# Self-attention scores of the second batch from stacked high and low parts (48 rows a head), one decoder layer on one core

## The chip, the cores and the metric

The kernel runs on one NeuronCore of a Trainium2 chip. The metric is the device time of one execution in microseconds (us), as a median of several runs. The engines are named PE (TensorE, matrix products), DVE (VectorE), ACT (ScalarE), POOL (GpSimd) and SP (SyncE, which here only issues DMAs). They run their own instruction streams in order and wait for each other through semaphores.

## The reference

One pre-norm decoder layer in float32, for x of shape (2, 256, 256): causal self-attention with 16 heads of 16, an attention over a context of 512 tokens, and a mixture of 16 experts of which 4 count for each token.

```python
def _L0_attn_ref(X, Wq, bq, Wk, bk, Wv, bv, Wo, bo):
    scale = 1.0 / np.sqrt(np.sqrt(16))
    Q = (X @ Wq.T + bq).reshape(B, S, 16, 16) * scale
    K = (X @ Wk.T + bk).reshape(B, S, 16, 16) * scale
    V = (X @ Wv.T + bv).reshape(B, S, 16, 16)
    scores = jnp.einsum('bqhd,bkhd->bhqk', Q, K)
    scores = jnp.where(causal, scores, -jnp.inf)
    attn = jax.nn.softmax(scores, axis=-1)
    return jnp.einsum('bhqk,bkhd->bqhd', attn, V).reshape(B, S, 256) @ Wo.T + bo

x = x + attn(layernorm(x))
x = x + context_attention(layernorm(x), ctx_2048, mask)
x = x + experts(layernorm(x))
```

## The kernel before

Everything stays in SBUF; DMAs bring inputs and expert weights. The core does the projections, then self-attention in 16 steps, then context attention, then 16 experts.

**High and low parts.** Most products are not taken in float32. Each operand is split into a high part (rounded to float32r, the format of the names kh, qh, XH, WHg) and a low part (the rest, kl, ql, XL, WLg), and a product is the sum of three: high by high, low by high, high by low. The keys' high parts are written by ACT (L419), their low parts by POOL (`low_keys`, L321); the queries' high parts by ACT (L424), their low parts by DVE (L623).

**The 16 steps.** A step v takes two heads j = 0, 1 of one batch: steps 0 to 7 are the first batch, 8 to 15 the second. Two steps make a group of four heads. Heads are 16 wide and lie two by two in strips of 32 partitions. The queries are stored twice, each copy with zeros over one head of every strip (`parity`), so a product over the 32 rows of a strip gives one head's scores. PE, ACT and DVE each have a loop over v:

- PE: `scores(v)`, then `turn(v-1)` (transposes of the exponentials), and in odd steps `values` (the product with V). Scores are for the 256 queries of a batch in two blocks of 128: the first block sees 128 keys and is one float32 product (L970), the second sees 256 keys and is the three part products (L974). The two heads lie in different strips of the array and their products run side by side.
- DVE: mask and row maximum (L718, two instructions and two read-outs per head), then the copy of one head's turned exponentials out of PSUM (L743), besides other work that is placed at fixed steps.
- ACT: the exponentials (L438, four per step), the copy of the other head (L486), in odd steps the copy of a group's output (L493).

Scores of step v go to one of three pairs of PSUM banks, and the turned exponentials of step v take the same banks, so `scores(v)` waits for the copies of step v-3 (`pt_done`). `turn(v-1)` waits for the exponentials of step v-1 (`exp_done`).

From step 10 on the first batch's output is also finished inside these steps: `turn_back` (L1008), `outputs` (L649, L650), the transposes of att (L904), `project` (L1017), `residual` (L656), `centre` (L664 to L668). After step 15 follow the context scores (L1029) with their row maximum (L681).

**Order by hand.** There is no scheduler: each engine's order is the code's. POOL does constants, the sum xb (L301), the keys' low parts, then the splits of the first two experts' weights (L356, L308, L360, L315), of the router (L340, L342) and of the context (L350, L352), the mask (L331, L334) and from then on the reciprocal deviations (`rstds`, L296). SP issues all input DMAs but three, the last being dbias (L247), and then waits in a loop for buffers of expert weights (L253, L255).

Of the kernel before, what the change touches and what calls it, by code (L numbers as in the profile page):

```python
# [36 lines left out]
DW = D * KD  # L37

# [4 lines left out]
def decoder_layer(nc, x_d, ctx_d, ctxT_d, wqkv_d, wo_d, params_d, rows_d, mask_d, dbias_d, we_d, out_d):  # L43
    ctx = ExitStack()
    with ctx:
# [7 lines left out]


# [98 lines left out]
        qh, ql = ([X[1][:, m, :].rearrange("p (r b q) -> p r b q", r=2, b=B) for m in range(KD)] for X in (HH, HL))  # L153
        q2 = [qpar[:, m, :, :].rearrange("p r (b c q) -> p r b c q", b=B, c=QC)[:, :, :, QC - 1, :] for m in range(KD)]
# [45 lines left out]
        out_done = sem("out_done")  # L200

# [32 lines left out]
        def _(sp):  # L234
# [12 lines left out]
            sp.dma_start(dbias[:, :], dbias_d).then_inc(dbias_in, 16)  # L247
            with sp.Fori(1, E // 2) as pair:
# [13 lines left out]
        def _(pool):  # L262
# [27 lines left out]
            g.memset(vp[:, :, :, DH:HP], 1.0)  # L290

# [69 lines left out]

            low_keys(0)
# [26 lines left out]
        def _(act):  # L389
# [75 lines left out]
            for v in range(NV + 2):  # L465
# [6 lines left out]
                if v == NV - 2:  # L472
# [5 lines left out]
                    a.activation(pt[:, w // 2 % 2, 2 * (w % 2), :, :].rearrange("p c q -> p (c q)"),  # L478
                                 PS[:, 2 * (w % 3), 0:BLK * P], ACT.Copy).then_inc(pt_done[0], 1)
                if 1 <= v <= NV:  # L480
# [5 lines left out]
                    a.activation(pt[:, w // 2 % 2, 2 * (w % 2) + 1, :, :].rearrange("p c q -> p (c q)"),  # L486
# [80 lines left out]
        def _(dve):  # L567
# [141 lines left out]
            for v in range(NV + 2):  # L709
# [27 lines left out]
                if 1 <= v <= NV and v != NV - 2:  # L737
# [5 lines left out]
                    v_.tensor_copy(pt[:, w // 2 % 2, 2 * (w % 2), :, :].rearrange("p c q -> p (c q)"),  # L743
# [152 lines left out]
        def _(pe):  # L896
# [56 lines left out]
            def scores(v):  # L953
# [4 lines left out]
                if v in (0, 4):  # L958

                    pe.wait_ge(kl_done, g + 1)  # L960
                    pe.wait_ge(ql_done, g + 1)
                if v == 2:
                    pe.wait_ge(k_done, KD)
                if v >= 3:
# [3 lines left out]
                tiles = [slice(HP * (2 * pair + j), HP * (2 * pair + j + 1)) for j in range(2)]  # L968
# [280 lines left out]
```

## Time and profile before

| what | value |
|---|---|
| median of 3 runs | 222.13 us (221.68 to 222.31) |
| the profiled execution, its own time | 221.69 us |
| its span | 219.6 us |
| PE busy | 212.3 us (97%) |
| DVE busy | 159.5 us (73%) |
| ACT busy | 129.7 us (59%) |
| POOL busy | 84.2 us (38%) |
| DMA | 17.41 MB, mean 79 GB/s |

The span is the stretch between the first and the last instruction that the profiler saw; the execution's own time is 2.1 us longer. PE's busy time is modelled, and matmuls overlap, so 97% does not mean that PE has no room. The granted clock was full speed (2.4 GHz) in all 40 slices of the page.

### The profile page before, as it was taken

The numbers are of one execution on the slowest core, as the hardware profiler recorded it, in microseconds if no ns is written. First come the engines' busy times: TensorE is split into PE (matmuls) and PEld (weight loads), VectorE is DVE, ScalarE is ACT, GpSimd is POOL, SyncE is SP. The second block draws the span as 40 slices with busy tenths as digits, with TensorE's granted clock in tenths as the row PEclk, the third lists the DMA queues.
The fourth block names the chain that finished last, engine by engine and source line by source line (L and its number), as shares of the span: only waits on it lengthen the run. The fifth ranks groups of instructions, "written<-read, shape, count | busy, mean of one in ns | idle before, by whom it ended". The sixth has DMA issues, their size and how long they took to land.

```text
span 219.6 us, 4392 instructions
## 1 busy us (share of the span) xinstructions
PE 212.3 (97%) x1394; PEld 176.9 (81%) x1394; DVE 159.5 (73%) x438; ACT 129.7 (59%) x248; POOL 84.2 (38%) x70
## 2 busy tenths in 40 slices
PE   7999999998999999999999999999999999999995
PEld 2688766776776789788898898898898898898893
DVE  3579897879468558898895785785786786786754
ACT  2238789859632714656765665675676666666340
POOL 6259989201002010246535615615516516416000
PEclk9999999999999999999999999999999999999999
DMA  6994420000000000031442142142241241310002
GB/s 181 328 383 152 145 100 0 0 4 0 3 0 0 3 0 1 0 87 61 145 143 87 60 143 72 72 143 54 89 143 40 103 143 28 115 48 0 0 0 96
DMA packets 7997, 17.41 MB, mean 79 GB/s; under 512 B 928, under 2 KB 3120, under 8 KB 7856
## 3 DMA queue, kind: packets, MB, share of 16 engines
q1 hardware_dynamic: 7552, 16.94, 23.7%
q10 hardware_dynamic: 432, 0.31, 0.5%
q8 instruction: 7, 0.11, 0.2%
q14 instruction: 6, 0.05, 0.1%
HBM read 16.72 MB, written 0.52 MB: 79 GB/s over the span
## 4 chain that ended last, share of the span: by engine, by line
PE 88%; DVE 5%; ACT 3%; issue 3%; POOL 1%; DVEq 0%; ACTq 0%; POOLq 0%
PE PS L1160 37%; PE PS L1176 20%; PE PS L932 3%; PE PS L1044 3%; PE PS L1029 3%; PE PS L984 3%; PE PS L920 2%; PE PS L1127 2%; ACT pr L438 2%; PE PS L1017 2%; PE PS L946 2%; PE PS L970 2%; PE PS L1205 2%; PE PS L997 2%; PE PS L974 1%
## 5 line engine op out<-in xcount | busy, mean ns | idle before, releaser
L308 POOL TENSOR_TENSOR WLg<-raw_g,WHg 128x1024 fp32r<-128x1024 f32 x16 | 38.3, 2396 | 70.8 <-ACT WHg L408 70.6
L1160 PE MATMUL PS<-XH,WHg 128*128 128x512 f32 x120 | 47.0, 391 | 0.0
L1160 PE MATMUL PS<-XL,WHg 128*128 128x512 f32 x120 | 46.9, 391 | 0.0
L1160 PE MATMUL PS<-XH,WLg 128*128 128x512 f32 x120 | 46.7, 389 | 0.0
L840 DVE TENSOR_SCALAR pt<-pt 128x512 f32<-128x512 f32 x30 | 25.0, 833 | 22.4 <-ACT pt L532 22.4
L1176 PE MATMUL PS<-WHd,HH 128*128 128x256 f32 x120 | 34.0, 283 | 0.0
L1176 PE MATMUL PS<-WLd,HH 128*128 128x256 f32 x120 | 34.0, 283 | 0.0
L1176 PE MATMUL PS<-WHd,HL 128*128 128x256 f32 x120 | 34.0, 283 | 0.0
L532 ACT ACTIVATE pt<-PS,bup 128x512 f32<-128x512 f32 x30 | 20.7, 688 | 15.2 <-PE PS L1160 15.2
L538 ACT ACTIVATE HH<-pt 128x512 fp32r<-128x512 f32 x30 | 18.9, 629 | 16.1 <-DVE pt L844 15.7
L438 ACT ACTIVATE pr<-masked,nmax 128x128 f32<-128x128 f32 x64 | 23.7, 444 | 5.9 <-DVE nmax L718 5.9
L529 ACT ACTIVATE pt<-PS,params 128x512 f32<-128x512 f32 x30 | 20.6, 688 | 10.8 <-PE PS L1160 10.8
L1160 PEld LDWEIGHTS PS<-XH,WLg 128*128 128x128 f32 x120 | 22.5, 188 | 4.8
L1160 PEld LDWEIGHTS PS<-XH,WHg 128*128 128x128 f32 x120 | 22.6, 188 | 4.2
L1160 PEld LDWEIGHTS PS<-XL,WHg 128*128 128x128 f32 x120 | 22.6, 188 | 4.1
L844 DVE SCALAR_TENSOR_TENSOR pt<-pt 128x512 f32<-128x512 f32 x30 | 22.4, 746 | 4.2 <-ACT pt L529 2.0
L833 DVE SCALAR_TENSOR_TENSOR x<-PS,score,x 128x256 f32<-128x256 f32 x60 | 24.8, 476 | 0.0
L1176 PEld LDWEIGHTS PS<-WHd,HH 128*128 128x128 f32 x120 | 23.0, 191 | 0.9 <-issue 0.3
L1176 PEld LDWEIGHTS PS<-WHd,HL 128*128 128x128 f32 x120 | 23.0, 191 | 0.5
L1176 PEld LDWEIGHTS PS<-WLd,HH 128*128 128x128 f32 x120 | 23.0, 191 | 0.0
L718 DVE CUSTOM_DVE_ANT_0 masked<-PS,causal 128x128 f32<-128x128 f32 x64 | 18.9, 353 | 4.2 <-PE PS L974 4.2
L849 DVE TENSOR_TENSOR HL<-pt,HH 128x512 fp32r<-128x512 f32 x30 | 20.6, 688 | 1.4
(162 smaller groups left out, 355.8 us busy)
## 6 DMA issues: line engine op xcount, KB each, us to landing
raw_g<-we_d SPq DMA_DIRECT2D x16, 512.0 KB, 4.0
raw_w<-we_d SPq DMA_DIRECT2D x16, 256.0 KB, 2.7
ctxT<-ctxT_d SPq DMA_DIRECT2D x1, 1024.0 KB, 10.4
ctx_sb<-ctx_d SPq DMA_DIRECT2D x1, 1024.0 KB, 12.5
wqkv<-wqkv_d SPq DMA_DIRECT2D x3, 256.0 KB, 4.9
out_d<-x SPq DMA_DIRECT2D x4, 128.0 KB, 1.8
rows<-rows_d SPq DMA_DIRECT2D x1, 264.0 KB, 6.3
x<-x_d ACTq DMA_DIRECT2D x2, 128.0 KB, 3.0
```

The lines of the kernel that those rows point to most:

```text
L308: g.tensor_tensor(WLg[slot][:, :, :, :].rearrange("p k g f -> p (k g f)"), raw_g[slot][:, :], WHg[slot][:, :, :, :].rearrange("p k g f -> ...
L438: i = a.activation(pr[:, v % 2, j, cols], masked[:, v % 2, j, cols], ACT.Exp, bias=nmax[:, v % 2, j, qc:qc + 1], scale=-1.0)
L529: a.activation(glu[:, m, :], PS[:, 2 * m, :], ACT.Gelu_apprx_sigmoid, bias=gub[:, bass.ds(e, 1), 0, m]).then_inc(glu_done, 1)
L532: a.activation(upc[:, m, :], PS[:, 2 * m + 1, :], ACT.Identity, bias=bup1[:, bass.ds(e, 1), m]).then_inc(up_done, 1)
L538: a.activation(HH[slot][:, m, :], hid[:, m, :], ACT.Copy).then_inc(hh_done, 1)
L718: i = v_.tensor_tensor_reduce(out=masked[:, v % 2, j, cols], in0=PS[:, 2 * (v % 3) + j, cols], in1=causal[:, cols], scale=1.0, scalar=HUGE ...
L833: v_.scalar_tensor_tensor(out=acc[:, c, :], in0=PS[:, 4 + 2 * slot + c // 2, (c % 2) * D:(c % 2 + 1) * D], scalar=score[:, c, bass.ds(e, 1 ...
L840: v_.tensor_scalar(upc[:, m, :], upc[:, m, :], 1.0 - LIMIT, 1.0 + LIMIT, ALU.max, ALU.min).then_inc(upc_done, 1)
L844: v_.scalar_tensor_tensor(out=hid[:, m, :], in0=glu[:, m, :], scalar=GLU_MAX, in1=upc[:, m, :], op0=ALU.min, op1=ALU.mult).then_inc(hid_do ...
L849: v_.tensor_tensor(HL[slot][:, m, :], hid[:, m, :], HH[slot][:, m, :].bitcast(F32), ALU.subtract).then_inc(hl_done, 1)
L1160: i = t.matmul(PS[:, 2 * m + part, :], w[slot][:, k, part, m * P:(m + 1) * P], xx[:, k, :], start=(n == 0), stop=(n == 3 * KD - 1))
L1176: i = t.matmul(PS[:, 4 + 2 * slot + c // 2, (c % 2) * D:(c % 2 + 1) * D], hh[slot][:, k, c * P:(c + 1) * P], w[slot][:, k, :], start=(n == ...
```

## The change

Only the second batch's scores (steps 8 to 15) are computed in another way. For each of its heads the 16 rows of the three operand parts are stacked in 48 partitions: keys as low, high, high, and queries as high, high, low. One product over 48 rows is then the sum of the three. Heads 0 to 3 of a group of eight stand in partitions 0 to 47, heads 4 to 7 in 64 to 111, in the free dimension one after another. The first block of 128 queries is taken from the same stacks and is no longer a float32 product. The stacks are built by way of DRAM, by SP: six DMAs write the parts of 8 heads, and after all six have landed four DMAs read them back into `raw_ks` and `raw_qs`; this is done for each half m of the heads. POOL then rounds the stacks into `ks` and `qs` (the same memory) with two casts for each half, and PE waits for them in steps 8 and 12. POOL also clears `raw_ks` and `raw_qs` at the start. Queries of the second batch are no longer stored twice; their high and low parts get instructions of their own. In the first batch the two heads of a step come from strips 0 and 2 or 1 and 3, and no longer from 0 and 1 or 2 and 3.

```diff
+            sp.wait_ge(parts_zero, 2)
+            for m in range(KD):
+                sp.wait_ge(kl_done, m + 1)
+                for a, part in enumerate((kl[m], kh[m], kh[m])):
+                    sp.dma_start(k_parts[m, :, a], part[:, S:T].bitcast(F32)).then_inc(parts_out, 16)
+                sp.wait_ge(ql_done, 2 * m + 2)
+                for a, part in enumerate((qh1[m], qh1[m], ql1[m])):
+                    sp.dma_start(q_parts[m, :, a], part.bitcast(F32)).then_inc(parts_out, 16)
+                sp.wait_ge(parts_out, (m + 1) * 2 * PARTS3 * 16)
+                for rows_of, parts in ((raw_ks, k_parts), (raw_qs, q_parts)):
+                    for j in range(2):
+                        sp.dma_start(rows_of[64 * j:64 * j + PARTS3 * DH, m * NG:(m + 1) * NG, :],
+                                     parts[m, j * NG:(j + 1) * NG].rearrange("t a d n -> (a d) t n")).then_inc(parts_in[m], 16)
...
+            g.memset(raw_ks[:, :, :], 0.0).then_inc(parts_zero, 1)
+            g.memset(raw_qs[:, :, :], 0.0).then_inc(parts_zero, 1)
...
+            def take_parts(m):
+                pool.wait_ge(parts_in[m], 4 * 16)
+                for whole, raw in ((ks, raw_ks), (qs, raw_qs)):
+                    g.tensor_copy(whole[:, m * NG:(m + 1) * NG, :], raw[:, m * NG:(m + 1) * NG, :]).then_inc(parts_done, 1)
...
             low_down(0, 0)
+            take_parts(0)
             high_gate_up(1)
             low_gate_up(1, 1)
+            take_parts(1)
             split_router()
...
             def high_queries(m):
-                act.wait_ge(q_done, m + 1)
-                for r in range(2):
-                    i = a.activation(qh[m][:, r], q2[m][:, r], ACT.Copy)
-                i.then_inc(qh_done, 1)
+                act.wait_ge(q_done, 2 * m + 1)
+                a.activation(qh[m], q2[m], ACT.Copy).then_inc(qh_done, 1)
+                act.wait_ge(q_done, 2 * m + 2)
+                a.activation(qh1[m], q1[m], ACT.Copy).then_inc(qh_done, 1)
...
                 for r in range(2):
-                    i = v_.tensor_scalar(qpar[:, m, r, :], PS[:, Q_BANK[m], :], bq[:, m:m + 1], parity[:, r:r + 1], ALU.add, ALU.mult)
+                    i = v_.tensor_scalar(qpar[:, m, r, 0:S], PS[:, Q_BANK[m], 0:S], bq[:, m:m + 1], parity[:, r:r + 1], ALU.add, ALU.mult)
                 i.then_inc(q_done, 1)
+                v_.tensor_scalar(q1[m], PS[:, Q_BANK[m], S:T], bq[:, m:m + 1], -DH ** -0.25, ALU.add, ALU.mult).then_inc(q_done, 1)
 
             def low_queries(m):
-                dve.wait_ge(qh_done, m + 1)
-                v_.tensor_tensor(ql[m], q2[m], qh[m].bitcast(F32), ALU.subtract).then_inc(ql_done, 1)
+                for n, (low, q, high) in enumerate(((ql[m], q2[m], qh[m]), (ql1[m], q1[m], qh1[m]))):
+                    dve.wait_ge(qh_done, 2 * m + n + 1)
+                    v_.tensor_tensor(low, q, high.bitcast(F32), ALU.subtract).then_inc(ql_done, 1)
...
+                if v in (2 * NG, 3 * NG):
+                    pe.wait_ge(parts_done, 2 * g + 2)
...
+                if b == 1:
+                    whole = [slice(64 * j, 64 * j + PARTS3 * DH) for j in range(2)]
+                    t4 = g * NG + pair * 2 + r
+                    for out, tile in zip(outs, whole):
+                        t.matmul(out[:, P:BLK * P], qs[tile, t4, P:S], ks[tile, t4, :], start=True, stop=True)
+                    for out, tile in zip(outs, whole):
+                        t.matmul(out[:, 0:P], qs[tile, t4, 0:P], ks[tile, t4, 0:P], start=True, stop=True).then_inc(sc_done, 1)
+                    return
```

On PE, step 8 (the first of the second batch) and the turn of step 7 before the change; each row is an instruction with its destination, sources and size:

```order
L970 MATMUL PS<-kT,qpar 128x128 [waits pt_done1,pt_done0]
L970 MATMUL PS<-kT,qpar 128x128
L974 MATMUL PS<-HH 128x256 x2
L974 MATMUL PS<-HH,HL 128x256 x2
L974 MATMUL PS<-HL,HH 128x256 x2
L984 MATMUL PS<-ident,pr 128x128 [waits exp_done]
```

The same place on PE after the change:

```order
L1012 MATMUL PS<-ks,qs 128x256 [waits pt_done1,pt_done0,parts_done]
L1012 MATMUL PS<-ks,qs 128x256
L1014 MATMUL PS<-ks,qs 128x128 x2
L1031 MATMUL PS<-ident,pr 128x128 [waits exp_done]
```

Eight products became four, and the first of them waits for POOL's casts as well.

On POOL, the place behind the low part of the first expert's down weights, after the change (before it, the casts into ks and qs are not there, and the rest follows in the same order):

```order
L343 TENSOR_TENSOR WLd<-raw_w,WHd 128x512 [waits whd_done]
L394 CAST ks<-raw_ks 128x1024 [waits parts_in0]
L394 CAST qs<-raw_qs 128x1024
L384 CAST WHg<-raw_g 128x1024 [waits raw_g_in1]
L336 TENSOR_TENSOR WLg<-raw_g,WHg 128x1024 [waits whg_done]
L394 CAST ks<-raw_ks 128x1024 [waits parts_in1]
L394 CAST qs<-raw_qs 128x1024
L368 CAST router_parts<-params 128x2x16 [waits param_in]
```

Four casts entered POOL's order, two of them in front of the second expert's weights, and the splits of router, context and mask moved behind all four.

## Rows read from the trace of the kernel before

**Rows 1.** The page: busy us, share of the span and instructions of each engine.
```profile
PE 212.3 (97%) x1394; PEld 176.9 (81%) x1394; DVE 159.5 (73%) x438; ACT 129.7 (59%) x248; POOL 84.2 (38%) x70
```

**Rows 2.** Timeline of PE: start us, length us, engine, line, operation, count.
```profile
33.27 0.49 PE L970 MATMUL PS<-kT,qpar 32*128 32x128 f32 x4
33.52 0.37 PE L974 MATMUL PS<-HH 32*128 32x256 f32 x2
33.72 0.29 PE L974 MATMUL PS<-HH,HL 32*128 32x256 f32 x2
33.84 0.29 PE L974 MATMUL PS<-HL,HH 32*128 32x256 f32 x2
34.05 0.88 PE L984 MATMUL PS<-ident,pr 128*128 128x128 f32 x6
...
37.64 0.49 PE L970 MATMUL PS<-kT,qpar 32*128 32x128 f32 x4
```

**Rows 3.** Timeline of ACT, steps 8 to 10 (in brackets: idle time before, its releaser).
```profile
34.83 1.49 ACT L438 ACTIVATE pr<-masked,nmax 128x128 f32<-128x128 f32 x4
...
36.59 1.48 ACT L438 ACTIVATE pr<-masked,nmax 128x128 f32<-128x128 f32 x4
...
38.35 0.36 ACT L493 ACTIVATE osum<-PS 128x256 f32<-128x256 f32 x1
39.20 1.49 ACT L438 ACTIVATE pr<-masked,nmax 128x128 f32<-128x128 f32 x4 [0.48 <-DVE nmax L718]
```

**Rows 4.** Timeline of DVE, step 10, and the context's first row maximum.
```profile
38.52 0.29 DVE L718 CUSTOM_DVE_ANT_0 masked<-PS,causal 128x128 f32<-128x128 f32 x1 [1.12 <-PE PS L974]
...
56.31 0.69 DVE L681 CUSTOM_DVE_ANT_0 qpar<-PS,pen 128x512 f32<-128x512 f32 x1 [1.38 <-PE PS L1029]
```

**Rows 5.** The chain that ended last, in order of time, steps 10 to 16.
```profile
38.13 0.40 PE PS L974 x5
...
40.38 0.43 DVE att L650
...
43.55 0.42 PE PS L970 x4
...
54.45 1.69 PE PS L1029 x6
```

**Rows 6.** Timelines of PE and of DVE up to the first step's maximum.
```profile
15.70 0.29 PE L974 MATMUL PS<-HL,HH 32*128 32x256 f32 x2
...
16.13 0.29 DVE L718 CUSTOM_DVE_ANT_0 masked<-PS,causal 128x128 f32<-128x128 f32 x1
```

**Rows 7.** Timeline of POOL.
```profile
3.66 0.95 POOL L290 MEMSET vp<- 128x1024 f32 x1
9.54 2.81 POOL L301 TENSOR_TENSOR xb<-x,rows 128x256 f32<-128x256 f32 x4 [4.93 <-DMA rows<-rows_d]
...
23.14 1.03 POOL L356 CAST WHg<-raw_g 128x1024 fp32r<-128x1024 f32 x1
...
26.56 0.21 POOL L340 CAST router_parts<-params 128x32 fp32r<-128x32 f32 x1
...
37.52 2.37 POOL L352 TENSOR_TENSOR keys_low<-ctxT,keys_high 128x1024 fp32r<-128x1024 f32 x1
```

**Rows 8.** Stretches: us and length, busy of each engine, granted clock, DMA share, GB/s.
```profile
0.00:5.00 5.00, 3.62 (x9) 1.35 (x10) 1.42 (x4) 1.28 (x1) 3.48 (x17) 1.00 0.59 168
18.00:20.00 2.00, 2.00 (x21) 1.57 (x20) 2.00 (x7) 2.00 (x7) 1.92 (x2) 1.00 0.41 143
```

**Rows 9.** The page: packets, MB, share of 16 engines; KB and us to landing.
```profile
q1 hardware_dynamic: 7552, 16.94, 23.7%
...
out_d<-x SPq DMA_DIRECT2D x4, 128.0 KB, 1.8
```

**Rows 10.** Timeline of SP: start and length of issues.
```profile
5.50 0.55 SPq L242 DMA_DIRECT2D raw_w<-we_d  x1
8.51 3.62 SPq L247 DMA_DIRECT2D dbias<-dbias_d  x1
```

More of the change, by code:

```diff
@@ L37 @@
 DW = D * KD
+STEPS = 2 * NG
+PARTS3 = 3
 def decoder_layer(nc, x_d, ctx_d, ctxT_d, wqkv_d, wo_d, params_d, rows_d, mask_d, dbias_d, we_d, out_d):
@@ L52, in decoder_layer @@
         PS = ctx.enter_context(nc.psum_tensor("PS", [P, 8, 512], F32))
+        raw_parts = ExitStack()
+        raw_ks, raw_qs = (raw_parts.enter_context(nc.sbuf_tensor(n, [P, STEPS, S], F32)) for n in ("raw_ks", "raw_qs"))
+        raw_parts.close()
+        ks, qs = (sb(n, [P, STEPS, S], F32R) for n in ("ks", "qs"))
+        k_parts, q_parts = (nc.dram_tensor(n, (KD, G8, PARTS3, DH, S), F32, kind="Internal").ap() for n in ("k_parts", "q_parts"))
         first_use = ExitStack()
@@ L152, in decoder_layer @@
         kh, kl = ([X[0][:, m, :] for m in range(KD)] for X in (HH, HL))
-        qh, ql = ([X[1][:, m, :].rearrange("p (r b q) -> p r b q", r=2, b=B) for m in range(KD)] for X in (HH, HL))
-        q2 = [qpar[:, m, :, :].rearrange("p r (b c q) -> p r b c q", b=B, c=QC)[:, :, :, QC - 1, :] for m in range(KD)]
+        qh, ql = ([X[1][:, m, 0:2 * P].rearrange("p (r q) -> p r q", r=2) for m in range(KD)] for X in (HH, HL))
+        qh1, ql1 = ([X[1][:, m, S:T] for m in range(KD)] for X in (HH, HL))
+        q2 = [qpar[:, m, :, S - P:S] for m in range(KD)]
+        q1 = [qpar[:, m, 0, S:T] for m in range(KD)]
         keys_flat = qpar[:, :, :, :].rearrange("p k r t -> p (k r t)")
@@ L200, in decoder_layer @@
         out_done = sem("out_done")
+        parts_zero, parts_out, parts_done = sem("parts_zero"), sem("parts_out"), sem("parts_done")
+        parts_in = [sem(f"parts_in{m}") for m in range(KD)]
         XS_BANK, XT_BANK, XV_BANK = (7, 2, 4, 5), (3, 4, 6, 3), (1, 2, 4, 5)
@@ L477, in _ @@
                     act.wait_ge(pt_done[0], w)
[L478 removed]
+                    a.activation(pt[:, w // 2 % 2, w % 2, :, :].rearrange("p c q -> p (c q)"),
                                  PS[:, 2 * (w % 3), 0:BLK * P], ACT.Copy).then_inc(pt_done[0], 1)
@@ L967, in scores @@
                 outs = [PS[:, 2 * (v % 3) + j, :] for j in range(2)]
-                tiles = [slice(HP * (2 * pair + j), HP * (2 * pair + j + 1)) for j in range(2)]
+                if b == 1:
[6 more added lines that the diff above has]
+                    return
+                tiles = [slice(HP * (pair + 2 * j), HP * (pair + 2 * j + 1)) for j in range(2)]
                 for out, tile in zip(outs, tiles):
-                    t.matmul(out[:, 0:P], qpar[tile, g, r, b * S:b * S + P], kT[tile, g, b * S:b * S + P],
-                             start=True, stop=True)
+                    t.matmul(out[:, 0:P], qpar[tile, g, r, 0:P], kT[tile, g, 0:P], start=True, stop=True)
                 for n, (q, k) in enumerate(((qh, kh), (ql, kh), (qh, kl))):
                     for out, tile in zip(outs, tiles):
-                        i = t.matmul(out[:, P:BLK * P], q[g][tile, r, b, :], k[g][tile, b * S:(b + 1) * S],
+                        i = t.matmul(out[:, P:BLK * P], q[g][tile, r, :], k[g][tile, 0:S],
                                      start=(n == 0), stop=(n == 2))
@@ L1067, in _ @@
                 if v == 3:
-                    pe.wait_ge(q_done, KD)
+                    pe.wait_ge(q_done, 2 * KD)
                     project_values(1)
```

6 lines of the change are left out of this document (3 added, 3 removed).

## Prediction

> **What bounds the kernel now.** I read the page first: PE is marked busy for 97% of the span [rows 1], which looks as if every product removed were time gained. Its busy time is modelled, though, so the second view is the timelines of PE, ACT and DVE side by side over steps 8 to 10, and the question at each gap is who waits for whom. A step's scores hold PE from 33.27 to 34.05, 0.78 us [rows 2]. DVE starts on them 0.88 after they began (37.64 to 38.52 in step 10) [rows 2, 4], ACT's exponentials start 0.68 after that (39.20) [rows 3]. ACT itself has no idle time in steps 8 and 9: exponentials at 34.83 and 36.59, the output copy until 38.71; only before 39.20 does it wait, 0.48 us for DVE [rows 3]. So the steps run as a ring (scores, maximum, exponentials, turn, scores), in which ACT is nearly the bound. The chain of waits in order of time is the third view: from step 10 to the context scores at 54.45 it goes through PE and through DVE (att at 40.38) by turns [rows 5]. After 54.45 nothing is changed, and what is gained there should be carried to the end.
>
> **The change, part by part.**
>
> *Scores of steps 8 to 15.* Eight products become four. Before, the part products of 256 columns for two heads follow each other at 0.20 and 0.12 us (33.52, 33.72, 33.84), and the last pair takes 0.29 from its start [rows 2]. After, a pair of 256 columns comes first and the pair of 128 starts 0.12 to 0.20 behind it and ends 0.28 later; DVE picks up 0.03 after that. So DVE starts 0.43 to 0.52 after PE, where it was 0.88; I take 0.48, a gain of 0.40 per step on the path from PE to DVE. On PE itself some 0.4 of 0.78 go. No row shows a product over 48 rows nor one of 128 columns in float32r; bounds are 0 (if such pairs ran one after the other and at a slower rate, they would last as long as what they replace) and 0.53 (below). Added over eight steps this would be 3.2 us, and nearly all of it is hidden:
>
> - Steps 8 and 9: DVE's maximum would be earlier, but the exponentials cannot be, as ACT has work without a gap until 38.71. Gain 0. The turns and the values product wait for those exponentials, so step 10's scores start at 37.64 as before.
> - Step 10: DVE starts at 37.64 + 0.48 = 38.12 instead of 38.52, and ACT at 38.80 instead of 39.20; ACT is free at 38.71. Gain 0.40.
> - Steps 11 to 15: now DVE's order binds. Its maximum of step 11 stands behind the finished outputs of the first batch (att at 40.38 in the chain [rows 5]), which themselves moved by the same 0.40; later it stands behind the residual rows, then behind the centring. PE waits in between for ACT's copy of the turned att. Each of these instructions is unchanged, so the shift of 0.40 is handed on and not added to: scores that come earlier wait for a busy DVE. Even with the shortest products the shift can't pass some 0.53, since PE's turn of step 9 waits for exponentials that end at 38.07 (36.59 + 1.48) [rows 3], and the first batch's turning back stands behind it.
>
> *Prologue.* DVE writes the queries in three instructions of 256 columns instead of two of 512, and the low parts in two instead of one. The first step's products end at 15.70 + 0.29 = 15.99, DVE takes them at 16.13 without idle time [rows 6]: DVE was late by 0.1 at most. Gain 0 to 0.1; I take 0.05.
>
> *Clearing the stacks.* Two memsets of 2048 columns, twice 0.95 each: 3.8 us, in POOL's idle 4.93 us before xb [rows 7]. Cost 0; were the cover gone, the excess would delay the keys' low parts and so step 0.
>
> *DMAs.* SP's new DMAs stand behind dbias, whose issue took 3.62 us, so the queue is full there, and before the loads of experts 2 and on, whose buffers are wanted only in the expert stage. The write of one part is 128 runs of 1 KB. In the first 5 us, where such runs are loaded, 0.59 of 16 engines moved 168 GB/s [rows 8]: 17.8 GB/s each, 0.057 us for 1 KB. Call that p. The mean packet of the queue took 0.237 x 16 x 219.6 / 7552 = 0.110 us for 2.2 KB [rows 9], so p lies between 0.05 and 0.11; I take 0.057, as the row with the same size. What a write needs besides is 1.8 - 8 x 0.057 = 1.3 us from the row of out_d [rows 9]. The engines are full of loads until about 18.2 (share 0.41 in 18 to 20) [rows 8]. The writes' DRAM side has 8 as its outermost size; whether 8 or 16 engines carry one no row shows, and I reckon with 8, the slower.
> First half: 768 packets over 8 engines 96p = 5.5, landed at 18.2 + 5.5 + 1.3 = 25.0. Four reads: issues of 0.55 each [rows 10] make 2.2, the last one's data 12p = 0.7, and 1.3: 29.2. POOL, at its place since 23.14, waits 6 us, then two casts of 1.03 [rows 7]: 31.3. PE needs them at 33.27: 2.0 to spare.
> Second half: SP is free at 27.2; 0.55 + 5.5 + 1.3 + 4.2 bring it to 38.8; casts to 40.9. Needed in step 12, at 43.55 - 0.4 = 43.1 [rows 5]: 2.2 to spare.
> *POOL behind them.* Router, context and mask splits took from 26.56 to 39.89, 13.3 us: they end at 54.2. The first batch's context keys are needed at 54.0 and are among the first of these; the reciprocal deviation behind all of them is needed by DVE before its maximum at 56.31 - 0.4 [rows 4, 7]. 1.7 remain for one small instruction. Cost 0.
>
> **Sum.** 0.40 + 0.05 = 0.45 off the profiled execution's 221.69 gives 221.24. That execution lies 0.44 under the median of the runs, and a comparison is made with medians: 222.13 - 0.45 = 221.7.
>
> **The rivals.**
>
> *The stacks come late (slower).* With p free, the first half is ready at 25.1 + 108p and the second at 29.2 + 204p. The second is late from p = 0.068, the first from 0.076; at p = 0.080 step 12 starts 2.4 late, everything after it as well: 222.13 - 0.45 + 2.4 = 224.1. At the queue's mean of 0.110 it would be 8.5 late. For it: the two round trips are in series, and the margin is 2 us of some 20. Against: the rows of 1 KB runs. It rests on the 8 engines: with 16 the second half is ready at 29.2 + 108p, in time even at 0.110.
> The Trainium skill, page "DMA: Bandwidth & Descriptors", section "Why a DMA increments its semaphore by 16 and not by 1", says that a DMA goes over the largest number of engines up to 16 that divides the outermost size of both sides. By that rule the writes go over 8 engines and the reads over 16; no row here shows it.
>
> *Nothing gained.* Pairs over 48 rows don't run side by side, or 128 columns of float32r are as slow as float32's, which took 0.25 for the pair (33.27 to 33.52) [rows 2]. Then DVE starts 0.6 to 0.9 after PE, and the time is 222.1. For it: no row has this form. Against: pairs over 32 rows do run side by side, 512 columns in 0.12 us.
> The Trainium skill, page "TensorEngine Tiling (Array Packing)", section "Tiling Modes", has two independent tiles of 64 rows; by it the pairs run side by side and this rival falls.
>
> *PE counts after all (faster).* In the chain PE's scores stand again in step 12 (43.55) [rows 5], and the ring's even steps (10, 12, 14, and 16's context scores) could each give 0.4: 222.13 - 4 x 0.4 = 220.5. For it: PE's share of the span. Against: the walk above, where DVE is busy when those scores come.
>
> **How the numbers follow.** A measurement of this kernel tells 0.3% (0.67 us) from no change: faster is below 221.5, slower above 222.8. My forecast of 221.7: 0.32. Nothing gained, 222.1: 0.15. PE counts after all, 220.5: 0.28. Stacks late, 224.1: 0.20, with 0.05 more for a POOL that ends later than reckoned. So faster 0.29 (with 0.01 from the edge of the forecast), same 0.46, slower 0.25. The forecast's own range is 221.5 to 222.1; the range for 8 in 10 runs from 220.5 to 223.6, which leaves out most of the late stacks.
>
> **What the profile after would show.** Right: DVE's first maximum of step 10 starts near 0.48 after its scores; ACT still without a gap in steps 8 and 9; DVE without idle time before its maxima of steps 11 to 15; context scores at 54.0; POOL's first cast into ks at about 29, the third at about 39; no wait of PE for POOL in steps 8 and 12. Wrong: PE idle in step 8 or 12 with a cast as releaser (late stacks); DVE starting 0.6 or more after the new products (nothing gained); DVE idle before its later maxima and context scores before 53.4 (PE counts).

## The result, and the profile after

| what | before | after |
|---|---|---|
| median of 6 runs each, same chip | 222.01 us (221.60 to 222.31) | 226.78 us (224.34 to 227.45) |
| ratio, with its 95% interval | | 1.0195 [1.0154, 1.0235] |
| the profiled execution, its own time | 221.69 us | 224.34 us |
| its span | 219.6 us | 222.6 us |
| granted clock over the span | 1.00 (profiled execution) | 0.992 in two runs (224.34, 224.51), 0.983 to 0.985 in four (226.63 to 227.45) |

The change makes the kernel slower by 4.8 us. The prediction said 221.7, within 220.5 to 223.6; even the fastest run lies outside. The profiled execution is one of the two short ones, so it shows a loss of 2.65 us only. No run near the median was profiled, and the experiments had to stand in for it.

The page after, first the head and the busy times [rows 1], then the granted clock in the 40 slices:

```profile
span 222.6 us, 4327 instructions
PE 210.9 (95%) x1346; PEld 175.3 (79%) x1346; DVE 162.4 (73%) x442; ACT 129.9 (58%) x248; POOL 91.3 (41%) x76
PEclk9799999999999999999999999999999999999999
```

PE has less work (48 records and 1.4 us less; a float32 product leaves two records) and the execution is longer. The digit to stop at is the 7 in the granted clock's second slice; before, all 40 were 9.

**The prologue.** DVE's timeline after, from the layer norm to its first copy (start us, length us, engine, line, operation, count; in brackets idle time before and its releaser):

```profile
3.57 1.52 DVE L614 BATCH_NORM_STATS2 stats<-x 128x6 f32<-128x256 f32 x4 [3.57 <-DMA x<-x_d]
5.13 0.38 DVE L637 BATCH_NORM_AGGREGATE mv<-stats 128x2 f32<-128x6 f32 x4
6.17 3.03 DVE L629 TENSOR_SCALAR xn<-x,mv,rstd 128x256 f32<-128x256 f32 x4 [0.67 <-ACT rstd L436]
```

POOL's timeline after, the same stretch:

```profile
3.65 0.95 POOL L316 MEMSET vp<- 128x1024 f32 x1
4.55 1.80 POOL L317 MEMSET raw_ks<- 128x2048 f32 x1
6.29 1.80 POOL L318 MEMSET raw_qs<- 128x2048 f32 x1
```

Four instructions into xn take 3.03 us, where they took 1.38 before (the row `6.06 1.38 DVE L593` of that trace). DVE is shown as busy, not as idle, so no view of waits names the cause. Taken one by one, one of the four lasts 2.07 us and the others some 0.40; it is the first, since 8.24 to 9.20 is just the time of the other three. It was held from 6.17 to the end of POOL's second memset at 8.09, past the change of memsets at 6.3. PE pays for it, as its timeline after shows:

```profile
8.39 1.90 PE L942 MATMUL PS<-ident,xn 128*128 128x128 f32 x8 [2.03 <-DVE xn L629]
10.21 2.13 PE L970 MATMUL PS<-xT,wqkv 128*128 128x256 f32 x5
...
18.10 0.60 PE L1018 MATMUL PS<-kT,qpar 32*128 32x128 f32 x6
```

and the stretches of that time (us and length, busy of PE, weight load, DVE, ACT and POOL with counts, granted clock, DMA share, GB/s):

```profile
9.00:10.00 1.00, 1.00 (x7) 0.89 (x5) 0.21 (x1) 0.53 (x1) 0.46 (x1) 0.50 1.06 410
10.00:11.00 1.00, 1.00 (x4) 0.73 (x3) 0.68 (x2) 0.07 (x1) 1.00 (x3) 0.50 1.03 412
```

The transposes start at 8.39 instead of 6.62, 1.77 late. After the 2.03 us in which PE stood still the granted clock is 0.50 (1.2 GHz) from 9 to 11 us and 0.57 from 11 to 12, and the lateness grows to 2.96: step 0's scores start at 18.10, not 15.14. The clock's share of this is 1.19 us, since in a_again (below), the same program, the transposes also start at 8.39, the clock stays at 1.00 and step 0 starts at 16.91.

**The changed stage.** PE's timeline after, the scores of step 8 and of step 10 [rows 2]:

```profile
36.26 0.38 PE L1012 MATMUL PS<-ks,qs 48*128 48x256 f32 x2
36.48 0.22 PE L1014 MATMUL PS<-ks,qs 48*128 48x128 f32 x2
...
40.45 0.39 PE L1012 MATMUL PS<-ks,qs 48*128 48x256 f32 x2
40.67 0.22 PE L1014 MATMUL PS<-ks,qs 48*128 48x128 f32 x2
```

DVE's, step 10 [rows 4], and further on where it finishes the second layer norm's first half:

```profile
40.93 0.29 DVE L756 CUSTOM_DVE_ANT_0 masked<-PS,causal 128x128 f32<-128x128 f32 x1 [0.95 <-PE PS L1014]
...
54.22 0.54 DVE L704 TENSOR_SCALAR ve<-mv 128x2 f32<-128x2 f32 x1
54.68 0.60 DVE L706 TENSOR_SCALAR xn<-x,mv 128x256 f32<-128x256 f32 x2
```

POOL's, the first cast of either half and the last big instruction of its list [rows 7]:

```profile
29.96 1.04 POOL L394 CAST ks<-raw_ks 128x1024 fp32r<-128x1024 f32 x1 [4.89 <-DMA raw_qs<-q_parts]
...
40.08 1.04 POOL L394 CAST ks<-raw_ks 128x1024 fp32r<-128x1024 f32 x1 [4.67 <-DMA raw_qs<-q_parts]
...
52.38 2.36 POOL L380 TENSOR_TENSOR keys_low<-ctxT,keys_high 128x1024 fp32r<-128x1024 f32 x1
```

and PE's, where it waits for that xn, and the context scores [rows 5]:

```profile
55.08 0.70 PE L942 MATMUL PS<-ident,xn 128*128 128x128 f32 x4 [1.47 <-DVE xn L706]
...
57.19 0.50 PE L1076 MATMUL PS<-keys_high,XH 128*128 128x512 f32 x1
```

Step 10 came out to the hundredth: DVE starts 0.48 after its scores. But ve, which took 0.17 (`51.66 0.17 DVE L666` before), takes 0.54 and ends when POOL's subtraction into keys_low ends, at 54.74. It is the same picture as in the prologue, small here.

This table puts the profiled executions side by side. The stage runs from step 8's scores to the context scores; the rest from there to PE's last group of products (213.32 before, 216.05 after). The last six rows are experiments, told below.

| kernel | step 0's scores | stage | rest | own time |
|---|---|---|---|---|
| before | 15.14 | 33.27 to 54.45, 21.18 | 158.87 | 221.69 |
| after | 18.10 | 36.26 to 57.19, 20.93 | 158.86 | 224.34 |
| a_again (after once more) | 16.91 | 35.08 to 57.91, 22.83 | 158.84 | 225.14 |
| a_late | 15.43 | 35.18 to 59.19, 24.01 | 159.01 | 226.61 |
| a_warm | 16.91 | 35.07 to 59.37, 24.30 | 159.54 | 227.27 |
| a_holes8 | 15.10 | 33.25 to 54.95, 21.70 | 159.20 | 222.63 |
| a_holes16 | 15.25 | 33.41 to 54.17, 20.76 | 158.90 | 221.54 |
| b_short | 15.33 | 33.49 to 54.09, 20.60 | 158.87 | 221.35 |

In the changed kernel's profile the second column holds the whole loss: step 0 is 2.96 late, and from step 8 on nothing more is lost. In a_late and a_warm the stage itself is 2.8 and 3.1 longer. Two rows have a term beside these: in a_late step 8 comes 19.75 after step 0, where before it was 18.13, and a_warm's rest is 0.67 longer. Undisturbed, the new stage is 0.42 shorter (21.18 to 20.76).

### The profile page after: what moved, and what is told of

Read it like the earlier page. It is cut to its first block, busy times and chain, and to the rows that moved or that the text cites. A ratio compares the mean times of both kernels' runs of the same rounds, so it can differ in the third digit from the quotient of the medians.

```text
span 222.6 us, 4327 instructions
## 1 busy us (share of the span) xinstructions
PE 210.9 (95%) x1346; PEld 175.3 (79%) x1346; DVE 162.4 (73%) x442; ACT 129.9 (58%) x248; POOL 91.3 (41%) x76
## 4 chain that ended last, share of the span: by engine, by line
PE 84%; DVE 7%; ACT 3%; issue 3%; DMA 1%; POOL 0%; DVEq 0%; ACTq 0%
PE PS L1207 37%; PE PS L1223 19%; PE PS L970 4%; PE PS L1091 3%; PE PS L1076 3%; PE PS L1031 3%; PE PS L1174 2%; ACT pr L474 2%; PE PS L942 2%; DVE masked L756 2%; PE PS L1064 2%; PE PS L984 2%; PE PS L1252 2%; PE PS L1044 2%; DVE xn L629 1%
```

## The experiments

The theory they led to: while POOL works on SBUF, a `TENSOR_SCALAR` or `TENSOR_TENSOR` of DVE that reads and writes only SBUF is held up until POOL's work has ended. The change adds such POOL work in the prologue and pushes old POOL work to where DVE's critical small instructions stand. The rivals were that the loss lies in one of the two places alone, or in the new products and DMAs. The quoted expectations were written at different times and each speaks of the theories as they then stood.

**a_late: the memsets out of the prologue.** They go behind the keys' low parts, and SP waits for them only before the reads.

```diff
-            sp.wait_ge(parts_zero, 2)
...
                 sp.wait_ge(parts_out, (m + 1) * 2 * PARTS3 * 16)
+                sp.wait_ge(parts_zero, 2)
...
-            g.memset(raw_ks[:, :, :], 0.0).then_inc(parts_zero, 1)
-            g.memset(raw_qs[:, :, :], 0.0).then_inc(parts_zero, 1)
...
             low_keys(1)
+            g.memset(raw_ks[:, :, :], 0.0).then_inc(parts_zero, 1)
+            g.memset(raw_qs[:, :, :], 0.0).then_inc(parts_zero, 1)
```

> The changed kernel, its two memsets moved behind POOL's second low part of the keys, where POOL later has 4.9 us idle; SP waits for them only before its reads. Theory A (a memset on POOL holds up DVE's normalisation, PE then has nothing to do and its clock falls): DVE's four xn instructions take 1.4 us again instead of 3.0, PE's projections start at 8.1 instead of 10.2, the clock is full throughout, step 0 starts near 15.1, and the time is 221.4 to 222.0. Theory B (the DMAs, or the deeper prologue on DVE, cost the time): it stays near 225 to 227. Theory C (something later in the program costs it too): the prologue is repaired and the time stays over 222.8.

Measured: 226.72 us (226.50 to 227.38) against 221.84, ratio 1.0226 [1.0207, 1.0246]. The prologue is repaired (xn 1.38 again, clock 1.00, step 0 at 15.43), and nothing is won, because the loss moved. DVE's timeline of a_late:

```profile
53.15 2.27 DVE L704 TENSOR_SCALAR ve<-mv 128x2 f32<-128x2 f32 x1
```

POOL's:

```profile
51.92 1.04 POOL L376 CAST keys_high<-ctxT 128x1024 fp32r<-128x1024 f32 x1
53.04 2.35 POOL L378 TENSOR_TENSOR keys_low<-ctxT,keys_high 128x1024 fp32r<-128x1024 f32 x1
```

PE's, and the stretch after it:

```profile
55.73 0.82 PE L942 MATMUL PS<-ident,xn 128*128 128x128 f32 x4 [3.19 <-DVE xn L706]
```

```profile
56.00:60.00 4.00, 4.00 (x29) 2.74 (x28) 2.27 (x11) 2.73 (x7) 0.25 (x1) 0.57 0.00 0
```

Two numbers per partition take 2.27 us, from just after POOL's subtraction begins (53.04) to its end (55.39). PE stands still for 3.19 us and then has a clock of 0.57 for 4 us. So the prologue is one part of the cause, and a second meeting is another. The moved memsets also cost 1.6 us between step 0 and step 8, which is taken up with a_late16 below.

**b_clear: the kernel before, with the two memsets on arrays that nothing reads.**

```diff
+        raw_ks, raw_qs = (sb(n, [P, 8, S]) for n in ("raw_ks", "raw_qs"))
...
             g.memset(vp[:, :, :, DH:HP], 1.0)
+            g.memset(raw_ks[:, :, :], 0.0)
+            g.memset(raw_qs[:, :, :], 0.0)
```

> The kernel before, with nothing added but two arrays of 2048 columns and POOL's two memsets of them, behind the memset of vp. Theory A: DVE's first xn instruction lasts about 2 us, step 0's scores start 2.5 to 3.5 us later, the granted clock shows half speed in part of 8 to 15 us, and the time is 224.5 to 227.5, at least the whole loss. Theory B: 222.0.

Measured: 223.48 us (223.46 to 223.51), 1.0070 [1.0054, 1.0086], clock 1.00. DVE's timeline of b_clear, then PE's:

```profile
6.04 3.18 DVE L596 TENSOR_SCALAR xn<-x,mv,rstd 128x256 f32<-128x256 f32 x4 [0.67 <-ACT rstd L403]
```

```profile
8.40 1.31 PE L907 MATMUL PS<-ident,xn 128*128 128x128 f32 x8 [1.62 <-DVE xn L596]
```

xn is 1.80 longer, step 0's scores start at 16.92, 1.78 late, and the context scores 1.77 late (56.22): one term, handed through unchanged. That the two memsets alone cost 1.6 us is shown. It fell short of what was expected because the clock did not fall. PE's gap was 1.62 here and not 2.03, as the opening products on `warm` ended later; their end differs from execution to execution (a_again: a gap of 1.21).

**a_warm: 20 instead of 14 of the products that keep PE busy at the start.**

```diff
-            keep_warm(7, 14)
+            keep_warm(7, 20)
```

> The changed kernel with 20 instead of 14 warming products, which at 0.36 us each reach to about 8.5, so that PE has no gap before the transposes of xn. Theory A has two terms, the wait itself (2.1 us) and the lower clock behind it (0.9 us in the profiled run, some 3 more in the slower runs): the second goes, the clock is full throughout, the runs no longer fall in two groups, and the time is 223.4 to 223.9. If the clock falls for another reason than PE's gap, it stays 224.3 to 227.5 with two groups.

Measured: 227.65 us (227.27 to 227.72), 1.0258 [1.0242, 1.0275]. The expected 223.4 to 223.9 was far off. The clock held in the prologue and step 0 started 1.19 earlier than in the changed kernel (16.91); a_again has the same without the six products, so this edit doesn't show that they held the clock. Again nothing is won: DVE now reaches the second layer norm just when POOL's subtraction runs. DVE's timeline of a_warm:

```profile
53.03 0.17 DVE L704 TENSOR_SCALAR ve<-mv 128x2 f32<-128x2 f32 x1
53.11 2.71 DVE L706 TENSOR_SCALAR xn<-x,mv 128x256 f32<-128x256 f32 x2
```

POOL's subtraction ran from 53.05 to 55.40. PE stood still for 3.18 us and had 0.50 from 56 to 60. The two losses stand in for each other: who loses 1.2 us more in the prologue comes too late to lose them at the second meeting.

**b_short: the new products' shape without stacks.** On the kernel before, the second batch's scores are taken from the high parts alone, one product of 256 and one of 128 columns for each head; the two products with low parts are left out, and the first block uses the second block's queries. No DMAs, casts or memsets are added.

```diff
+                if b == 1:
+                    for out, tile in zip(outs, tiles):
+                        t.matmul(out[:, P:BLK * P], qh[g][tile, r, b, :], kh[g][tile, b * S:(b + 1) * S], start=True, stop=True)
+                    for out, tile in zip(outs, tiles):
+                        t.matmul(out[:, 0:P], qh[g][tile, r, b, :], kh[g][tile, b * S:b * S + P], start=True, stop=True).then_inc(sc_done, 1)
+                    return
```

> The kernel before; the second batch's scores are taken from the high parts alone, one product of 256 and one of 128 columns a head instead of four (the low parts' products are left out, and the first block uses the second block's queries). No stacks, DMAs or casts. This is the PE work of the change without its costs. Forecast's walk (ACT binds in steps 8 and 9, DVE from step 10): 0.3 to 0.5 us less than before, 221.5 to 221.7. Rival (PE counts): 1.6 us less or more, at most 220.5. Rival (nothing): 222.0.

Measured: 221.08 us (221.03 to 221.35), 0.9961 [0.9947, 0.9974]. PE's and DVE's timelines of b_short, step 10:

```profile
37.68 0.39 PE L971 MATMUL PS<-HH 32*128 32x256 f32 x2
37.91 0.22 PE L973 MATMUL PS<-HH 32*128 32x128 f32 x2
```

```profile
38.16 0.29 DVE L718 CUSTOM_DVE_ANT_0 masked<-PS,causal 128x128 f32<-128x128 f32 x1 [0.95 <-PE PS L973]
```

Again 0.48. The stage took 20.60, 0.58 less than before (step 8 happened to start 0.22 later, so the context scores came 0.36 earlier, at 54.09). The walk said 0.40, PE's count 1.6. The profiled executions differ by 0.34; the medians by 0.76, and why this is 0.2 to 0.4 more than stage and walk say stays open. It is under half of the 1.6 of PE's count.

**a_late16 and a_late_order: make POOL end earlier, or go past the subtraction.** Both start from a_late. a_late16 turns the DRAM layout so that the writes' outermost size is 128; a_late_order puts the first reciprocal deviation ahead of the second context's split.

```diff
-        k_parts, q_parts = (nc.dram_tensor(n, (KD, G8, PARTS3, DH, S), F32, kind="Internal").ap() for n in ("k_parts", "q_parts"))
+        k_parts, q_parts = (nc.dram_tensor(n, (KD, G8, DH, PARTS3, S), F32, kind="Internal").ap() for n in ("k_parts", "q_parts"))
...
-                    sp.dma_start(k_parts[m, :, a], part[:, S:T].bitcast(F32)).then_inc(parts_out, 16)
+                    sp.dma_start(k_parts[m, :, :, a].rearrange("t d n -> (t d) n"), part[:, S:T].bitcast(F32)).then_inc(parts_out, 16)
...
```

```diff
             masks()
+            rstds(1)
             split_keys(1)
-            for n in range(1, 5):
+            for n in range(2, 5):
```

> a_late with the stacks' arrays in DRAM laid out as (8 heads, 16, 3, 256), so that both a part's write and the read of a stack have an outermost size divisible by 16; rows of a stack come in another order, the same for keys and queries. Theory A2 (in a_late and in the slower runs of the changed kernel POOL's late split of the second context keys holds up DVE's small instruction ve at L704, PE idles 3 us and its clock falls): writes go over 16 engines, the stacks are ready 3 to 5 us earlier, POOL's second keys_low ends before 51, ve lasts 0.2 us, the clock is full, and the time is 221.3 to 221.7, as low as the forecast. If the engines' number doesn't follow from the layout, the stacks come as late as in a_late and the time stays at 226 to 227.5. If the loss is not from this collision, the time stays over 223 though POOL is early.

> a_late with POOL's first reciprocal deviation ahead of the split of the second context keys, so that this split cannot begin before DVE's ve; DMAs as in a_late. Theory A2: ve lasts 0.2 us, no idle 3 us on PE, full clock; the split now lies at 53 to 56.5, beside DVE's XL and xscale, which may wait up to 1 to 2 us of their own: 221.4 to 223.5. If the lateness of the stacks is the cause itself and not the collision: 226 to 227.

Measured: a_late16 223.36 us (222.74 to 224.55), 1.0073 [1.0048, 1.0097]; a_late_order 223.01 us (222.50 to 223.66), 1.0052 [1.0033, 1.0071]. In both ve takes 0.17 and 3.4 to 3.7 us of a_late's loss are gone. a_late16 missed its expected 221.3 to 221.7, and its time lies where the expectation put the case that the loss is not from the collision. Its trace says otherwise, as ve is short; what is left shows a third meeting, made by the moved memsets: they push the split of the gate weights to DVE's low query parts. DVE's timeline of a_late16, and POOL's:

```profile
21.91 2.93 DVE L661 TENSOR_TENSOR HL<-qpar,HH 128x256 fp32r<-128x256 f32 x2
```

```profile
22.03 2.53 POOL L334 TENSOR_TENSOR WLg<-raw_g,WHg 128x1024 fp32r<-128x1024 f32 x1
```

The changed kernel took 1.50 for the same pair and a_late 3.17. In a_late16 step 8 comes 1.4 us later after step 0 than before (19.50 to 18.13), about the 1.6 us that the median is over the kernel before. In a_late_order there is a fourth: `55.66 1.38 DVE L713 TENSOR_SCALAR xscale` (0.16 elsewhere) beside the subtraction at 54.63 to 57.02.

**b_split: the second meeting made in the kernel before.** POOL's split of the second context waits until the scores of step 14 are done; nobody needs it before some 68 us.

```diff
                     pool.wait_ge(v_ps, NC)
+                    pool.wait_ge(sc_done, 30)
```

> The kernel before, with POOL's split of the second context keys held back until step 14's scores are done (about 50.1), nothing else. Nobody needs the split before 68 us. Theory A2: keys_low runs from about 51.3 to 53.7 over DVE's ve at 51.66, which then lasts about 2 us instead of 0.17; xn, the transposes and the context scores come 2 us later, the clock may fall: 223.5 to 226.5. If POOL's work is harmless to DVE: 222.0.

Measured: 225.39 us (223.40 to 226.25), 1.0170 [1.0146, 1.0194]. One line, no product, DMA or byte added, and over 3 us lost. DVE's timeline of b_split, POOL's and PE's, and a stretch behind:

```profile
51.62 2.12 DVE L667 TENSOR_SCALAR ve<-mv 128x2 f32<-128x2 f32 x1
```

```profile
51.37 2.35 POOL L353 TENSOR_TENSOR keys_low<-ctxT,keys_high 128x1024 fp32r<-128x1024 f32 x1
```

```profile
54.05 0.70 PE L905 MATMUL PS<-ident,xn 128*128 128x128 f32 x4 [2.43 <-DVE xn L669]
```

```profile
53.00:56.00 3.00, 1.95 (x26) 1.48 (x26) 2.95 (x12) 1.35 (x5) 1.47 (x2) 1.00 0.00 0
```

The profiled execution (223.40) kept clock 1.00, though PE stood still for 2.43 us, and is 1.6 slower than the kernel before; the three others have 0.992 or 0.984 and are 3.4 to 4.5 slower. So the hold alone is worth some 1.6 us, and the executions with a lowered clock are 1.8 to 2.9 slower still. Their clock was read from the means of the runs, not from a trace, so that it fell behind this wait is likely and not shown.

**b_pieces: b_clear with each memset cut in four.** If DVE were let in between two instructions of POOL, short pieces would cost it little.

```diff
+        raw_ks, raw_qs = (sb(n, [P, 8, S]) for n in ("raw_ks", "raw_qs"))
...
             g.memset(vp[:, :, :, DH:HP], 1.0)
+            for raw in (raw_ks, raw_qs):
+                for i in range(4):
+                    g.memset(raw[:, 2 * i:2 * i + 2, :], 0.0)
```

> b_clear with each memset of 2048 columns cut in four of 512 (0.45 us each). If DVE waits for the end of one POOL instruction and can go between two of them: the first xn instruction lasts 0.4 to 0.9 us instead of 2.1, the delay shrinks to 0.3 to 1.2 us, and the time is 222.1 to 223.0. If DVE waits until POOL has no more such instruction queued, or both share the bandwidth: as b_clear, 223.5.

Measured: 223.69 us (223.65 to 224.68), 1.0080 [1.0061, 1.0099]. DVE's timeline of b_pieces, and POOL's:

```profile
6.08 3.37 DVE L597 TENSOR_SCALAR xn<-x,mv,rstd 128x256 f32<-128x256 f32 x4 [0.67 <-ACT rstd L404]
```

```profile
4.55 1.93 POOL L294 MEMSET raw_ks<- 128x512 f32 x4
6.42 1.93 POOL L294 MEMSET raw_qs<- 128x512 f32 x4
```

Cutting these memsets doesn't help: DVE was not let in between the pieces, as in the changed kernel it was not let in at 6.3, between the two memsets. They follow each other without a pause (each begins as the one before ends). Between a cast and a subtraction, which lie 0.09 us apart, DVE was let in: a_again below shows it. In the profiled execution, the one of 224.68, PE's gap grew to 2.35 and the clock fell as in the changed kernel (0.57 over 8 to 12 us).

**a_holes16 and a_holes8: POOL's work moved away from the DVE instructions that PE waits for.** From the changed kernel: one memset waits for xn, the other stands between the two low parts of the keys, the second half's casts go behind the router and the first context, and SP waits for the memsets only before its reads, as in a_late. a_holes16 also has a_late16's layout. Nothing is left out; this is a version that could be used.

```diff
-            g.memset(raw_ks[:, :, :], 0.0).then_inc(parts_zero, 1)
+            pool.wait_ge(xn_done, NC)
             g.memset(raw_qs[:, :, :], 0.0).then_inc(parts_zero, 1)
...
             low_keys(0)
+            g.memset(raw_ks[:, :, :], 0.0).then_inc(parts_zero, 1)
             low_keys(1)
...
-            take_parts(1)
             split_router()
             split_keys(0)
+            take_parts(1)
```

> The changed kernel with POOL's work moved out of the way of DVE's instructions on SBUF, and nothing left out: one memset waits for the normalised rows (7.4 to 9.3), the other stands in POOL's wait between the keys' two low parts (13.6 to 15.4); the router's and the first context keys' splits stand ahead of the second take of the stacks, so POOL's last split ends near 48, ahead of ve near 51.3; DRAM layout as in a_late16. Theory A (the whole loss is DVE held up by POOL on the way to SBUF, and the lower clock after it): xn 1.4 us, low query parts of the second half 0.8, ve 0.2, no gap of PE over 1.2 us, clock 1.00, context scores near 54.0, and the time is 0.3 to 0.6 us under the kernel before, 221.2 to 221.6. Rival (stacks have a cost of their own): 222.0 or more.

> a_holes16 with the change's own DRAM layout. The stacks are ready about 2 to 4 us later; POOL's last split ends near 51 to 52 and may still meet ve (up to 1 us, then 222.0 to 222.6), or just miss it (221.2 to 221.6). Writes from first issue to all landed: 7.4 us of the second half here, 5.8 in a_holes16, if the layout sets the number of engines.

Measured: a_holes16 221.54 us (221.39 to 221.84, 11 runs), 0.9989 [0.9980, 0.9998], clock 1.00 in every run. a_holes8 221.92 us (221.21 to 223.41, 12 runs), 1.0016 [0.9996, 1.0036]. DVE's timeline of a_holes16, POOL's and PE's:

```profile
6.17 1.38 DVE L630 TENSOR_SCALAR xn<-x,mv,rstd 128x256 f32<-128x256 f32 x4 [0.67 <-ACT rstd L437]
...
51.37 0.17 DVE L705 TENSOR_SCALAR ve<-mv 128x2 f32<-128x2 f32 x1
```

```profile
45.59 2.36 POOL L380 TENSOR_TENSOR keys_low<-ctxT,keys_high 128x1024 fp32r<-128x1024 f32 x1
```

```profile
54.17 0.50 PE L1077 MATMUL PS<-keys_high,XH 128*128 128x512 f32 x1 [0.17 <-DVE XL L745]
```

POOL is done at 47.95, the meetings that PE paid for are gone, and with the same products, DMAs, casts and memsets so are the 4.8 us. One meeting is left: the second half's low query parts still take 1.51 us (`21.35 1.51 DVE L662`) and not the expected 0.8, as in the changed kernel, and step 8 comes 18.16 after step 0, as there, so PE does not pay for it. This is what shows the cause: only POOL's order, SP's wait and the layout differ, and a_holes8, whose layout is the change's own, reaches 221.2 to 222.0 in most runs. It is the fastest version with the whole computation, 0.2 us under the kernel before, at the edge of what can be told apart. PE's last group starts 0.25 earlier than before, as the 0.28 at the context scores say.

a_holes8 has POOL end at 51.03, just in time for ve (0.17 at 51.21). Seven of its runs have clock 1.00 and 221.2 to 222.0; five have 0.992 and 222.6 to 223.4, the profiled one among them. There PE waited 1.08 us for xn (51.69), and the stretch behind it has a granted clock of 0.54:

```profile
53.00:56.00 3.00, 3.00 (x22) 1.68 (x21) 1.24 (x4) 2.36 (x7) 0.00 (x0) 0.54 0.00 0
```

It stands at the edge: b_short and a_holes16 waited 1.09 us at the same place and kept 1.00. In the changed kernel's own profile 1.47 us there left the clock at 1.00 as well, and in b_split's 2.43.

**a_again: the changed kernel once more, for the runs near 227.**

> The changed kernel once more, for a profile of its slower runs (four of six had a granted clock of 0.983 to 0.985 and 226.6 to 227.5 us). Theory A2: in such a run POOL's split of the second context keys begins before DVE's ve, ve lasts 1.5 to 2.5 us, PE idles 3 us or more before the transposes of xn at 54 to 56, and the clock falls a second time there. If the slower runs come from a longer cold stretch in the prologue, the lower clock is all before 20 us.

Measured: 225.98 us (225.14 and 226.82), 1.0186 [1.0153, 1.0219]. DVE's timeline of a_again, and POOL's:

```profile
53.05 0.18 DVE L704 TENSOR_SCALAR ve<-mv 128x2 f32<-128x2 f32 x1
53.13 1.39 DVE L706 TENSOR_SCALAR xn<-x,mv 128x256 f32<-128x256 f32 x2
```

```profile
53.27 1.10 POOL L378 CAST keys_high<-ctxT 128x1024 fp32r<-128x1024 f32 x1
54.46 2.37 POOL L380 TENSOR_TENSOR keys_low<-ctxT,keys_high 128x1024 fp32r<-128x1024 f32 x1
```

The same program with another course: PE's gap in the prologue was 1.21 and the clock stayed at 1.00 (step 0 at 16.91, as in b_clear and a_warm), DVE came to ve 1.17 us earlier, and its xn met the cast. PE stood still for 1.09 and then for 0.60 us, and the granted clock was 0.75 in the mean from 53 to 56 us and 0.76 from 56 to 60. The second of the two xn instructions ended at 54.52, 0.15 after the cast (54.37) and long before the end of the subtraction (56.83): here the hold ended with the one POOL instruction and did not go on over the next. This execution is 0.8 slower than the one with the lowered clock in the prologue. The expectation spoke of a run near 227 with ve held; this one is neither. Its lowered clock lies at the second meeting and not in the prologue, but no run near 227 of the changed kernel was profiled. What such a run loses, and where, is inferred and not shown: a_warm (227.3) has their mean clock of 0.983 from the second meeting alone, while one fall in the prologue and one at the second meeting, each of which gives 0.992 by itself (the execution of 224.34, a_late), would add up to it as well.

## Why the prediction was wrong, step by step

**"Clearing the stacks ... Cost 0" is the first step that failed.** It took POOL's idle time for free time. POOL was idle, and the memsets fitted (3.5 us in a gap of 4.9); but what stood beside them was DVE's xn, on which PE waits. They cost 1.77 us before step 0 (b_clear: 1.78) and, with the fall of the clock after PE's gap of 2.03 us, 2.96. In the trace of before one memset did run beside DVE, vp's at 3.66 [rows 7], and DVE's statistics took 1.42 (1.52 in the changed kernel). This is no leave for other instructions: statistics are not held, and xn is. The Trainium skill, page "SBUF — State Buffer", section "SBUF: two separate sides", says that VectorE and GpSimd share one pair of ports, which either locks for a whole instruction, and that it concerns VectorE's operations in a two-port mode, or with two inputs in SBUF against a GpSimd operation that reads SBUF. I had not weighed that rule. By it the meeting costs up to the length of POOL's instruction, as the rows of ve (2.27 beside 2.35) say. The trace goes further on one point: b_pieces and the first xn show a hold over several memsets without a pause between them, so that the price was all of them and not the rest of one. In a_again, between a cast and a subtraction, the hold did end with the one instruction.

**"POOL behind them ... Cost 0" is the second.** The working was right as far as it went: POOL's list was reckoned to end at 54.2 and ended at 54.74, and nobody who needs its results was kept waiting for long (`57.54 0.17 DVE L712`, 0.45 for rstd in a_again, is all there is in the four profiles with this order). What I did not ask is what DVE does while POOL is at work there. Before, POOL was idle from 39.89 to 51.91, and the layer norm's small instructions ran in that gap; the change filled the gap. This costs 0.2 to 0.4 us in the execution of 224.34 (stage 20.93, ve 0.37 longer), about 2 in a_again and more than 3 in a_late and a_warm (stages of 22.83, 24.01 and 24.30 against 20.76).

The two terms answer for the whole loss: a_holes16 has neither and is back at 221.5. That the runs of 226.6 to 227.5 divide it in one certain way between the two places is not shown.

**The scores term was right.** 0.48 us from scores to DVE was measured as 0.48; a gain of 0.40 over the stage, not 3.2, as 0.42 (a_holes16) and 0.58 (b_short). So "nothing gained" fell, 48 rows and 128 columns run side by side (the second pair starts 0.22 after the first and ends 0.22 after its own start), and "PE counts after all" fell with b_short: with half the products and nothing else changed the stage gave no 1.6 us. The prologue's 0.05 for the queries was nothing: DVE's first maximum starts 0.99 after step 0's first scores before and after (15.14 to 16.13, 18.10 to 19.09). In the time of the whole kernel the forecast gain of 0.45 was not seen in full either: a_holes16 is 0.2 under the kernel before.

**The DMAs were right, and the rival built on them fell.** The first half's casts were done at 31.98 (31.3 reckoned) and the second's at 42.09 (40.9 reckoned), and PE waited for neither. From the second half's first write to its reads took 33.80 - 26.39 = 7.41 us; reckoned with 8 engines were 7.35. That these agree so well is partly luck: the sum has one issue of 0.55, and SP's six issues took 3.66 (26.39 to 30.05). The two issue rows, on SP's timeline after:

```profile
26.39 0.59 SPq L265 DMA_DIRECT2D k_parts<-HL  x1
...
33.80 1.57 SPq L272 DMA_DIRECT2D raw_ks<-k_parts  x2
```

With the other layout the same stretch took 30.10 - 24.29 = 5.81 us in a_late16 and 5.67 in a_holes16; with the change's layout it was 7.80 in a_holes8, which differs from a_holes16 in the layout alone, and 8.09 in a_late. SP's issues make 0.7 of the difference (2.95 for the six in a_late16). A difference of 1.6 to 2.4 us is less than the 2.75 that half of 5.5 would be, but the sign is that of the Trainium skill's rule in "DMA: Bandwidth & Descriptors", section "Why a DMA increments its semaphore by 16 and not by 1": an outermost size of 8 leaves half of the engines out.

**The slower side was seen at the wrong place.** "Stacks late", and the 0.05 for a POOL that ends later, spoke of results that come late. The chances had no case in which an engine off the path slows one on it just by running.

## What to carry to other kernels

Idle time of POOL was free only where DVE at that moment worked on PSUM, took statistics or was idle itself: before an instruction is put into a gap, or old work is pushed along, lay DVE's timeline beside it and look for small instructions on SBUF that PE waits for. The hold shows as a long busy time of a short instruction and in no view of DVE's waits, so compare each instruction's length with the same instruction elsewhere (ve: 0.17 and 2.27 us). And when two kernels differ in where they lose, look at both places at once: here each repair of one place (a_late, a_warm) moved DVE into the other meeting and seemed to prove the place innocent.

## What the runs showed of the hardware that was not expected

- Some DVE instructions with source and destination in SBUF are held while POOL works: `TENSOR_SCALAR` of 128x256 to 2.07 us in the changed kernel and 2.44 in a_warm (0.34 to 0.40 alone), of 128x2 to 2.27 (0.17 alone), the pair of subtractions of 128x256 to 3.17 (a_late; 0.82 alone). Others are not: statistics and their aggregation, which also stay in SBUF, and everything that reads PSUM (row maximum, copies, XL) kept their lengths beside the same POOL instructions.
- The hold went on over memsets that follow each other without a pause: xn took 3.37 us with eight memsets of 0.5 us and 3.18 with two of 1.8. Between a cast and a subtraction 0.09 us apart DVE was let in (a_again).
- TensorE's granted clock fell to 1.2 GHz around or after stretches in which PE stood still for 2.03, 2.35, 3.18 and 3.19 us, and not with 1.62, 1.47 and, in b_split, 2.43. After 1.08 us at one place it fell in a_holes8, and with 1.09 followed by 0.60 in a_again, but with 1.09 it didn't in b_short and a_holes16. So the length of the wait alone does not decide, and what does is open. In the means of the runs a fall shows as 0.992 or 0.983 instead of 1.00.
- Products over 48 rows in two halves of the array run in pairs: 0.38 us for a pair of 256 columns and 0.22 for a pair of 128 in float32r.
